# Denominators of two head pairs in one pass of four 32-column tiles, in a fused attention and mixture-of-experts kernel

## What is computed

```python
q = (x @ Wq.T).reshape(b, t, 8, 64)
kv = x @ Wkv_down.T
k, v = (kv @ Wk_up.T), (kv @ Wv_up.T)          # 8 heads of 64
attn = softmax(einsum('bqhd,bkhd->bhqk', q, k) * 64 ** -0.5)
out = einsum('bhqk,bkhd->bqhd', attn, v).reshape(b, t, 512) @ Wo.T
x = x + ga * out                                 # the h that went in is layernorm(x) * (1 + ca) + sa
x = x + gb * ffn(layernorm(x) * (1 + cb) + sb)   # top 2 of 8 experts, capacity limited
```

## Time and profile before

| | |
|---|---|
| median of 3 runs | 1332.85 us (1331.63 to 1333.52) |
| the profiled execution | 1331.5 us, span of its instructions 1329.8 us |
| busy, share of the span | PE 87%, PEld 58%, DVE 73%, ACT 56%, POOL 70% |
| mean granted clock of PE | 0.927 of 2.4 GHz |

### The profile page before, as it was taken

How to read it: one execution, slowest core, us unless ns; L and a number is a source line. 1 busy time by engine, 2 the same in 40 slices (tenths; PEclk the granted TensorE clock), 3 DMA queues, 4 the chain that set the end, 5 groups by cost and what they waited for, 6 DMA issues and landing times. The chain is left out here.

```text
span 1329.8 us, 23668 instructions
## 1 busy us (share of the span) xinstructions
PE 1153.5 (87%) x5959; PEld 770.8 (58%) x5960; DVE 975.3 (73%) x2248; ACT 748.2 (56%) x1454; POOL 936.3 (70%) x1075
## 2 busy tenths in 40 slices
PE   7899999999999999999999999999987127889800
PEld 5556566666666565666666665656554025889800
DVE  4888686777777776777777777867675897567676
ACT  4566656576566656665655666566642431344436
POOL 4586969687878869697878779697865203546438
PEclk9899999999999999999999999999998555899955
DMA  4000101010101101010101010010102412314196
GB/s 155 16 20 17 48 18 49 17 64 1 64 16 48 48 16 48 16 62 2 64 1 64 16 48 33 17 33 17 49 1 79 113 63 67 61 33 111 27 304 205
DMA packets 68478, 70.91 MB, mean 53 GB/s; under 512 B 12912, under 2 KB 64032, under 8 KB 68272
## 3 DMA queue, kind: packets, MB, share of 16 engines
q1 hardware_dynamic: 46800, 47.18, 11.0%
q10 hardware_dynamic: 16896, 16.78, 3.8%
q0 software_dynamic: 4704, 6.11, 2.9%
HBM read 40.35 MB, written 29.45 MB: 52 GB/s over the span
## 5 line engine op out<-in xcount | busy, mean ns | idle before, releaser
L717 ACT ACTIVATE PF<-PS 128x512 f32<-128x512 f32 x512 | 298.4, 595 | 256.7 <-PE PS L1124 248.5
L1016 DVE TENSOR_REDUCE NMAX<-PS 128x1 f32<-128x512 f32 x512 | 342.6, 682 | 88.5 <-PE PS L1133 84.8
L579 POOL TENSOR_TENSOR SF<-SF,PF 128x512 f32<-128x512 f32 x252 | 323.2, 1304 | 14.0 <-ACT PF L717 13.8
L1205 PE MATMUL PS<-PF,V 128*64 128x512 f32 x1024 | 248.0, 605 | 0.0
L1123 PE MATMUL PS<-Q,K 128*128 128x512 f32 x512 | 221.9, 433 | 2.6 <-ACT PF L717 2.5
L1133 PE MATMUL PS<-K,Q 128*128 128x512 f32 x512 | 205.8, 404 | 11.0 <-DVE NMAX L1016 10.9
L1124 PE MATMUL PS<-Q,K 128*128 128x512 f32 x512 | 201.5, 394 | 0.0
L736 ACT ACTIVATE Q<-PS 64x512 fp32r<-64x512 f32 x256 | 151.7, 593 | 48.2 <-PE PS L172 43.3
L656 POOL TENSOR_TENSOR XL<-XF,XH 128x512 fp32r<-128x512 f32 x63 | 82.9, 1316 | 131.1 <-ACT XH L794 131.1
L576 POOL TENSOR_TENSOR SF<-PF 128x512 f32<-128x512 f32 x126 | 162.4, 1305 | 5.8 <-ACT PF L717 5.3
L1123 PEld LDWEIGHTS PS<-Q,K 128*128 128x128 f32 x512 | 96.4, 188 | 120.0 <-issue 55.2
(11 more groups left out here) (361 smaller groups left out, 2427.2 us busy)
## 6 DMA issues: line engine op xcount, KB each, us to landing
X<-in_L_attn_x SPq DMA_DIRECT2D x16, 512.0 KB, 3.3
MODB<-mod_rows SPq DMA_DIRECT2D x16, 512.0 KB, 3.6
h_rows<-H ACTq DMA_DIRECT2D x16, 512.0 KB, 3.0
acc_rows<-H ACTq DMA_DIRECT2D x16, 512.0 KB, 4.1
out_x<-X SPq DMA_DIRECT2D x16, 512.0 KB, 2.9
A<-acc_rows SPq DMA_DIRECT2D x15, 512.0 KB, 8.9
W1F<-in_L_ffn_W SPq DMA_DIRECT2D x3, 1024.0 KB
W2F<-in_L_ffn_W SPq DMA_DIRECT2D x3, 1024.0 KB
```

What stands on the lines that cost most here:

```text
L579: s_sum.done(pool.tensor_tensor(total, total, tile, ALU.add))
L717: s_exp.done(act.activation(PF[:, u % 8, :], st_bank(u), ACT.Exp))
L1016: s_mred.done(dve.tensor_reduce(NMAX[:, p % 2, r:r + 1], mx_bank(u), AX.X, ALU.max, negate=True))
L1205: last = pe.matmul(num_bank(p)[odd * R:(odd + 1) * R, :], V1[:, vp, c, :], PF[:, k % 8, :], start=(c == 0), stop=(c == TC - 1))
```

## The change

Two pairs of heads form a group g. After the sums of both pairs, one job den multiplies SF with a 128 x 32 matrix of ones, once for each of four heads, into partitions 32 x head to 32 x head + 31 of one bank: four tiles of 32 columns. There are two such jobs per batch, at slots 18 and 36, where there were four at 12, 20, 28 and 36. Job den now stands ahead of a slot's values, not behind them. DVE transposes the bank into XF once for both pairs, takes eight reciprocals of 32 x 16 into RDEN (128 x 2 x 16; each head's on two blocks of 32 partitions), transposes them back for one pair, then for the other, and multiplies. There is a new tile NUMS: ACT copies the values of the group's first pair from PSUM into it (KEEP_AT, slots 19 and 26), so that their bank comes free, and DVE multiplies NUMS with XF in place, both in SBUF; the second pair is multiplied from PSUM into XF as before. POOL's first add of pairs 2 and 3, and of the next batch's pairs 0 and 1, waits for the group before. PE's values wait for the copy (even pairs) or the multiply (odd pairs). XH and XL of the four pairs move to slots 22, 27, 39, 40 and one later. In the last batch pairs 2 and 3 are done one by one, pair 2 with 64-column tiles in a bank of its own.

Around it most constants of the order change, AHEAD from 13 to 14 among them. The diff, cut to its core:

```diff
-    XF, RDEN = sb("XF", [P, T]), sb("RDEN", [P, T // 32])
+    XF, NUMS, RDEN = sb("XF", [P, T]), sb("NUMS", [P, T]), sb("RDEN", [P, 2, T // 32])
...
-    AHEAD, PV_AT, ADD_LAG, DIV_AT, XH_AT, NORM_AT, MOD_AT, OUT_AT = 13, 4, 2, 12, 16, 19, 41, 63
-    STAT_AT, XN1_AT, XN2_AT, H2_AT, GBB_AT = (2, 6, 6, 9), (2, 2, 4, 5), (50, 51, 52, 53), (52, 55, 57, 59), (58, 62, 71, 72)
-    AT = {("mrow", 1): 4, ("mrow", 2): 12, ("mrow", 3): 20, ("mrow", 0): -4, ("den", 0): 12, ("den", 1): 20, ("den", 2): 28,
-          ("den", 3): 36, ("q", 0): -17, ("q", 1): -10, ("q", 2): -2, ("q", 3): 6, ("n1t", 0): -23, ("n1t", 1): -22,
-          ("lat", 0): -18, ("vt", 0): -15, ("proj", 0): 42, ("proj", 1): 45, ("proj", 2): 47, ("proj", 3): 48, ("h2t", 0): 58,
-          ("h2t", 1): 58, ("h2t", 2): 61, ("h2t", 3): 64, ("lg", 0): 66}
+    AHEAD, PV_AT, ADD_LAG, NORM_AT, MOD_AT, OUT_AT = 14, 4, 2, 19, 42, 67
+    XH_AT, FINAL_XH, FINAL_DEN, KEEP_AT = (22, 27, 39, 40), (23, 25, 32, 40), {2: 28, 3: 36}, (19, 26)
+    STAT_AT, XN1_AT, XN2_AT, H2_AT, GBB_AT = (0, 9, 12, 13), (3, 3, 4, 4), (48, 50, 51, 56), (52, 53, 56, 57), (53, 53, 70, 71)
+    AT = {("mrow", 1): 4, ("mrow", 2): 11, ("mrow", 3): 20, ("mrow", 0): -5, ("den", 0): 18, ("den", 1): 36, ("q", 0): -18,
+          ("q", 1): -12, ("q", 2): -4, ("q", 3): 6, ("n1t", 0): -23, ("n1t", 1): -23, ("lat", 0): -19, ("vt", 0): -18,
+          ("proj", 0): 43, ("proj", 1): 44, ("proj", 2): 44, ("proj", 3): 45, ("h2t", 0): 53, ("h2t", 1): 59, ("h2t", 2): 60,
+          ("h2t", 3): 62, ("lg", 0): 70}
-    LAG = {"mrow": 0, "proj": 1, "q": 3, "n1t": 1, "lat": 0, "vt": 1, "lg": 2, "h2t": 2, "den": 0}
+    LAG = {"mrow": 0, "proj": 1, "q": 3, "n1t": 1, "lat": 1, "vt": 2, "lg": 2, "h2t": 0, "den": 0}
...
                 if c == 1:
-                    s_den.wait(pool, b, p - 2)
+                    s_den.wait(pool, b, p // 2 - 1)
...
+                    for g, tb in due(KEEP_AT, b, n):
+                        if not (final(tb) and g):
+                            s_pv.wait(act, tb, 2 * TC * g + TC - 1)
+                            s_xlo.wait(act, tb - 1 + g, 2 - 2 * g)
+                            s_kept.done(act.activation(NUMS[:, :], num_bank(2 * g), ACT.Copy))
...
+            def normalise_group(xb, g, part, place):
...
+                if (part, place) == (0, 1):
+                    s_den.wait(dve, xb, g)
+                    s_xhi.wait(dve, xb, 2 * g - 1)
+                    s_xlo.wait(dve, xb, 2 * g - 1)
+                    s_x.done(dve.transpose(XF[:, :], job_bank(DENS[g])))
+                elif (part, place) == (1, 0):
+                    s_x.wait(dve, xb, base)
+                    for i in range(2):
+                        for k in range(4):
+                            head = slice((2 * i + k // 2) * 32, (2 * i + k // 2 + 1) * 32)
+                            s_x.done(dve.reciprocal(RDEN[k * 32:(k + 1) * 32, i, :], denominators(XF[head, :])))
+                elif (part, place) in ((1, 1), (2, 1)):
+                    s_x.wait(dve, xb, base + BACK[part - 1] - 1)
+                    s_x.done(back(XF[:, :], RDEN[:, part - 1, :]))
+                elif (part, place) == (2, 0):
+                    s_x.wait(dve, xb, base + BACK[0])
+                    s_kept.wait(dve, xb, g)
+                    s_x.done(dve.tensor_tensor(NUMS[:, :], NUMS[:, :], XF[:, :], ALU.mult))
+                elif (part, place) == (3, 0):
+                    s_x.wait(dve, xb, base + BACK[1])
+                    s_pv.wait(dve, xb, TC * (2 * g + 1) + TC - 1)
+                    s_x.done(dve.tensor_tensor(XF[:, :], num_bank(1), XF[:, :], ALU.mult))
...
+                        if kind == "den" and exists(b + off) and not (final(b + off) and g):
+                            wait_job_bank(pe, b, job)
+                            s_sum.wait(pe, b + off, 4 * (TC - 1) * (g + 1) - 1)
+                            for head in range(4):
+                                last = pe.matmul(job_bank(job)[head * 32:(head + 1) * 32, :], ONE[:, 0:32], SF[:, head // 2, head % 2, :],
+                                                 start=True, stop=True)
+                            s_den.done(last)
```

More of the change, by code:

```diff
@@ L420, in wait_job_bank @@
                 return
-            if banks[kind, idx, off] == banks[job] and exists(bb):
+            if banks[kind, idx, off] == banks[job] and exists(bb) and not (kind == "den" and idx and final(bb)):
                 stream, each, last = FREED[kind]
@@ L834, in final_scale, with back @@
                 dve.scalar_tensor_tensor(out=nmr, in0=mean, scalar=-1.0, in1=y, op0=ALU.mult, op1=ALU.mult).then_inc(done, 1)
-            def normalise(b, n, place):
-                xb, p = unit(b, n - DIV_AT)
-                p, part = p // 8, (n - DIV_AT) % 8
-                if not exists(xb):
-                    return
-                if (part, place) == (0, 1):
-                    s_den.wait(dve, xb, p)
+            def back(dst, reciprocals):
+                return dve.transpose(dst, reciprocals.unsqueeze(2).broadcast_to([P, T // 32, 32]))
@@ L845, in normalise, with normalise_pair @@
+            def normalise_pair(xb, p, part, place):
+                base = GROUP_OPS + 4 * (p - 2)
+                if (part, place) == (0, 1):
+                    s_den.wait(dve, xb, p - 1)
                     s_xhi.wait(dve, xb, p - 1)
                     s_xlo.wait(dve, xb, p - 1)
-                    den = final_den if final(xb) and p == H // 2 - 1 else job_bank(DENS[p])
-                    s_x.done(dve.transpose(XF[:, :], den))
+                    s_x.done(dve.transpose(XF[:, :], final_den[p - 2]))
@@ L855, in normalise @@
+                    s_x.done(back(XF[:, :], RDEN[:, 0, :]))
                 elif (part, place) == (2, 0):
-                    s_x.wait(dve, xb, 4 * p + 2)
+                    s_x.wait(dve, xb, base + 2)
                     s_pv.wait(dve, xb, TC * p + TC - 1)
                     s_x.done(dve.tensor_tensor(XF[:, :], num_bank(p), XF[:, :], ALU.mult))
+            def normalise(b, n, place):
+                for part in range(4):
+                    for g in range(2):
+                        at = AT["den", g] + part
+                        xb = b - at // UNITS
+                        if at % UNITS == n and exists(xb) and not (final(xb) and g):
+                            normalise_group(xb, g, part, place)
+                    for p, start_at in FINAL_DEN.items():
+                        at = start_at + part
+                        if at % UNITS == n and final(b - at // UNITS):
+                            normalise_pair(b - at // UNITS, p, part, place)
@@ L1216, in body @@
                                     s_den.done(last)
[L1217 to L1225 removed]
+                    if final(b) and n == FINAL_DEN[2]:
+                        s_mred.wait(pe, b, UNITS - 1)
+                        for odd in range(2):
+                            s_sum.wait(pe, b, 2 * (TC - 1) * 3 - 2 + odd)
+                            last = pe.matmul(final_den[0][odd * R:(odd + 1) * R, :], ONE[:, :], SF[:, 0, odd, :], start=True, stop=True)
+                        s_den.done(last)
             batches(pe, body)
```

77 lines of the change are left out of this document (43 added, 34 removed).

## The result

The change makes the kernel slower by 0.8%. The median of five runs is 1344.69 us (1340.72 to 1346.82), beside 1333.19 us (1331.63 to 1333.62, five runs) for the kernel before on the same chip: ratio 1.0081, 95% interval 1.0068 to 1.0094. The forecast was 1316 us in a range up to 1328, so the direction was wrong. The profiled execution took 1340.7 us, span 1339.0; the two spans lie 9.2 us apart, and that is the difference explained here. (The changed kernel's runs spread over 6 us; the rest of its median's 11.5 us isn't in the profile.)

What follows compares the result with a forecast made beforehand. PE was taken as the bound, so work saved there returns nearly whole: 1331.5 - 18.8 (PE's balance) + 2.3 (POOL wait less old hole) = 1315.0, plus 1.35 for the median, 1316 us. Own range 1310 to 1322, wider range 1303 to 1328.

Steps and rivals of the forecast that it cites:

- Denominators on PE: PE's denominator matmuls: eight records on four tiles take 0.86 us; 63 pairs cost 54.2 us before, 31 groups 26.7 after.
- Rival (c): PE's denominators: the four tiles run as two pairs, 1.72 us a group, 26.7 us more, 1342 us; chance 0.05.
- The switches: PE's tile-width changes: 0.33 us for entering and leaving at slot 18, 0.165 at slot 36; 5.3 and 2.5 us in all.
- DVE's burst: DVE, slots 19 to 23: eight reciprocals take 1.4 us; the chain of 7.05 us fits PE's 7.3 with 0.2 over.
- The old hole at slot 20: PE's late start of L1133 at slot 20, 0.65 us a batch, was to go and was credited.
- POOL's chain: POOL, slots 18 to 36: 26.0 us against PE's 25.2, charged 0.8 us a batch; less the old hole, 2.3 us given back.
- the 1.1 forecast: The forecast's gain for each steady batch of the attention, 1.1 us.
- The rest: SP's order, loads, the write of H from slot 63 to 67, and the last stretch: no cost charged.
- a dear tile: PE's denominators: Rival (c), four tiles running as two pairs, 1342 us; chance 0.05.
- a stretched POOL: POOL's chain: every second operation at 1.67 us in place of 1.25, 44 us more, 1360 us; chance 0.05.

Runs made afterwards that it cites:

- the kernel with two: The changed kernel with two reciprocals of 128 x 16 per group in place of eight, values divided by other heads' denominators, time only: 1329.17 us, ratio 0.9975.
- the group in the old order: The group of four 32-column tiles, its NUMS copies and new waits, with all other steps ordered as in the kernel before: 1451.1 us, ratio 1.0899.
- AHEAD 13: Row scores 13 units ahead, not 14, against the changed kernel with the write of H at slot 63 and the later multiply: 1361.32 us, ratio 1.0207.

## Why the prediction was wrong, step by step

- **Denominators on PE: right.** Four tiles run side by side, 1.00 us for a group where I took 0.86 and switches. Rival (c) is out.
- **The switches: right in kind, too dear alone.** Slot 18 lasts 1.78 us for 0.70 to 0.80 bare, so two switches cost 0.12 to 0.22 us and not 0.33. The one at slot 36 costs 0.14 us; I had 0.165. The Trainium skill, "TensorEngine Tiling (Array Packing)", Key Properties, says that a change of tiling mode drains the engine. The trace agrees as far as it goes: the step from values to denominators of the same width cost 0.04 us before (1.76 for 1.72).
- **DVE's burst: the step that failed in every batch.** "Eight take 1.4 to 2.0 us" and 1.4 in the sum, from the 0.17 us between a reciprocal and the NMAX behind it. That is the spacing of a reciprocal of 128 x 16, to an NMAX or to another such reciprocal; the eight are of 32 x 16, and from one to the next it is 0.27 (2.18 us for eight, above even the 2.0). The whole chain from the group to the NMAX that PE needs took 8.1 us where I had 7.05: 0.8 from the reciprocals, 0.15 from a slower start of the transpose, the rest in small gaps. PE came to need it after 7.2, so the hole is 0.90. Two reciprocals take 0.86 us off a batch; five take 0.57 off one that the later multiply had already shortened by 0.32.
- **The old hole at slot 20** went, as forecast.
- **POOL's chain: charged with 0.8 us, and not seen.** POOL goes from 500.82 to 526.02 us, 25.2 and not 26.0, and PE's way from one group to the next is 26.4 us (500.64 to 527.08), not 25.2, with the hole and longer bare slots in it. PE doesn't wait for SF at slot 36. NUMS x XF does stretch (0.69 us least, 1.86 at most), which no row shows as a cost. That the steady batch gains 0.77 us, not far from the 1.1 forecast, is luck in part: the 0.8 us that POOL didn't cost makes up for the 0.90 of the hole for NMAX.
- **The sum of a steady batch.** Denominators -1.46 (3.44 to 1.98), hole -0.65, new hole +0.90: -1.21, and -0.77 is measured. Of the 0.44 left, some lie in slots of 0.80 us where I counted 0.70; I didn't follow them further.
- **"The rest", costed at nothing: the step that failed at the edges,** for 16.4 us. The write of H: some 6 us by moving it back, 4.6 of them in batches 13 and 14. Holes of the last batch and the half clock behind them: 4.8. The start: 3.3 and 1.7, part of it a bank wait, most of it open. The end behind the last score, 2.7, comes with the group; how is open. I also multiplied a gain of the loop by 15, where 11 batches have it.
- **The sum of the miss.** Forecast were 16.5 us less in the span (1331.5 to 1315.0), measured 9.2 more, 25.7 apart: the edges 16.4, the gain of 1.1 us that four batches at the edges didn't have 4.4, the 0.33 missing in each of eleven steady batches 3.6, and 1.4 in the rest of the span. So the larger failure is that of the edges; without the hole that the reciprocals make, the steady batches would have paid for it (11 x 0.86 + 8.5 = 18 us; the kernel with two has a span of 1329.1 us, the kernel before 1329.8).
- **The chances.** I gave 0.10 to slower, all of it to a dear tile or a stretched POOL. A rival "the order's edges" was missing, though the earlier trace rows showed the last stretch at 40 of 57 us busy, thus full of chains that a moved slot can lengthen.

## What to carry to other kernels

The spacing of an instruction of one shape doesn't price another shape: a smaller reciprocal lasts as long as a large one (0.245 and 0.253 us) and, here, follows its like 0.1 us later. An unmeasured burst counts at the full length of each of its instructions, and where the slack is 0.2 us the pessimistic end is the forecast. A hand-written order has to be costed at its edges too: fill, the first bodies out of the loop, the last batch. And on a PE that is nearly always busy, a hole of two or three microseconds can be paid twice, when the granted clock falls with it, so the clock is read in one-microsecond windows wherever a batch is longer than its neighbours.

## What the runs showed of the hardware

- Eight 32 x 16 reciprocals take 2.18 us and four take 1.07: each starts 0.27 us after the last, when that one has ended. Two of 128 x 16 take 0.36: they start 0.17 us apart and overlap. One of 128 x 32 takes 0.35. Whether the number of partitions or the change of blocks keeps the small ones from overlapping isn't shown.
- Eight records on four tiles of 32 columns hold PE for 1.00 us.
- From 60 us to the last score, the fourteen traces have twelve holes of PE of 3.0 to 4.5 us, and with each the granted clock fell to 1.2 GHz, for 3.4 or 6.8 us. The hole of 2.36 us for NMAX in the last batch stands in ten kernels and went with a fall in seven; it did not with the write at slot 63, the later multiply and the five reciprocals. Of the shorter ones a few did, down to 1.65 us (the group in the old order), and most did not; nor did holes of 2.59 us (AHEAD 13) and 2.87 us (the transposes of H). The mean clock of the whole run, 0.922, 0.927 before, hardly tells.
- The first of two transfers issued on ACT's queue takes it 0.37 to 0.46 us, the second 0.38 to 1.62, mostly 0.40 to 0.53.
